# A decoder layer on one core: TensorE's state sums, D product and x transposes move between the transposes of an attention group, and ScalarE alternates copies with exponentials

## The reference

```
x = layernorm(x + attention(x))              # 16 heads of 16, causal
x = layernorm(x + ssm(ctx, z=x))             # selective state space, DI = 256, 16 states
x = layernorm(x + moe(x))                    # 8 experts, top 2, INTER = 512
```

```
u     = silu(conv(in_proj @ ctx) + conv_b)
delta = softplus(dt_proj @ (x_proj @ u)[:8] + b);   B, C = (x_proj @ u)[8:24], [24:40]
state[e,n] = state[e,n] * exp(delta[e,t] * A[e,n]) + delta[e,t] * u[e,t] * B[n,t]
y[e,t]     = sum_n state[e,n] * C[n,t]  +  D[e] * u[e,t]
out        = y * silu(z)
```

## Time and profile before

| | us |
|---|---|
| median of 3 runs | 490.91 |
| lowest, highest | 488.83, 492.13 |
| the profiled execution | 490.96 |
| its span, from the first instruction to the last | 489.2 |

### The profile page before, as it was taken

One profiled execution on the slowest core, in us unless ns is written; L12 is line 12 of the kernel. 1 busy time (PEld: TensorE's weight loads), 2 busy tenths in 40 slices (PEclk: granted clock), 3 DMA queues, 4 the chain that ended last, 5 costly groups with the idle time before them and its releaser, 6 DMA issues.

```text
span 489.2 us, 5425 instructions
## 1 busy us (share of the span) xinstructions
PE 356.7 (73%) x1783; PEld 214.0 (44%) x1783; DVE 266.5 (54%) x392; ACT 200.6 (41%) x459; POOL 195.1 (40%) x155
## 2 busy tenths in 40 slices
PE   5990568786868978689586653149999999999800
PEld 3440434353434734347353331125666666666500
DVE  4036465769985897869986754622222222222246
ACT  2258666863756655575565500012222222222100
POOL 2030324579463776357645442031333333332111
PEclk9995667989887976889777975559999999999965
DMA  6002001015111241014210714610111111111052
GB/s 189 0 5 86 21 3 44 21 44 194 45 43 44 62 175 40 25 44 148 68 45 21 232 48 171 237 43 11 54 46 43 43 45 44 44 52 46 22 182 86
DMA packets 29437, 34.45 MB, mean 70 GB/s; under 512 B 4058, under 2 KB 23810, under 8 KB 29410
## 3 DMA queue, kind: packets, MB, share of 16 engines
q1 hardware_dynamic: 27202, 28.07, 17.9%
q0 software_dynamic: 2208, 6.03, 4.2%
HBM read 28.92 MB, written 5.18 MB: 70 GB/s over the span
## 4 chain that ended last, share of the span: by engine, by line
PE 63%; DVE 14%; ACT 13%; issue 4%; DMA 2%; POOL 1%; DVEq 1%; SPq 0%; POOLq 0%; ACTq 0%
PE psS L1354 17%; PE psT L1192 7%; PE psY L1146 5%; ACT probT L628 5%; PE psY L1373 4%; PE psO L1373 4%; PE psS L1064 3%; PE psO L1203 3%; DVE experts L813 3%; PE psS L1120 2%; PE psB L1364 2%; PE psS L1234 2%; ACT experts L588 2%; DVE negmax L820 2%; ACT probs_at L620 2%
## 5 line engine op out<-in xcount | busy, mean ns | idle before, releaser
L461 POOL TENSOR_TENSOR experts<-experts,c_rows 128x1024 f32<-128x1024 f32 x32 | 75.3, 2352 | 108.4 <-DVE experts L813 108.4
L1354 PE MATMUL psS<-experts,delta 128*128 x184 | 88.7, 606 | 0.5 <-ACT delta L707 0.5
L813 DVE TENSOR_TENSOR_SCAN experts<-experts 128x1024 f32<-128x1024 f32 x32 | 78.1, 2439 | 1.7 <-ACT experts L588 0.6
L1192 PE MATMUL psT<-ident,probs_at 128*128 128x128 f32 x192 | 38.9, 337 | 30.1 <-ACT probT L628 22.4
L508 POOL DMA_INDIRECT z_out<-delta,row_out x23 | 22.7, 988 | 90.9 <-ACT delta L721 90.9
L588 ACT ACTIVATE experts<-delta,A_sb 128x255 f32<-128x255 f32 x128 | 54.8, 521 | 2.2 <-DVE du L787 2.2
L998 DVE COPY u_sb<-psB 128x512 f32<-128x512 f32 x23 | 15.9, 692 | 68.6 <-PE psB L1364 68.6
L464 POOL TENSOR_TENSOR experts<-experts 128x512 f32<-128x512 f32 x32 | 49.9, 1559 | 2.5
L628 ACT COPY probT<-psT 128x512 f32<-128x512 f32 x48 | 28.1, 586 | 48.2 <-PE psT L1192 47.4
L1146 PE MATMUL psY<-experts,ident 128*128 128x512 f32 x64 | 41.6, 739 | 7.6 <-POOL experts L464 7.5
L1354 PEld LDWEIGHTS psS<-experts,delta 128*128 128x128 f32 x184 | 33.8, 195 | 25.3 <-issue 24.2
(11 more groups left out here) (209 smaller groups left out, 547.7 us busy)
## 6 DMA issues: line engine op xcount, KB each, us to landing
c_rows<-c_dram SPq DMA_DIRECT2D x32, 256.0 KB, 3.4
experts<-in_L_ffn_w_gate_dram SPq DMA_DIRECT2D x8, 512.0 KB, 5.9
experts<-in_L_ffn_w_up_dram SPq DMA_DIRECT2D x8, 512.0 KB, 6.8
experts<-in_L_ffn_w_down_dram SPq DMA_DIRECT2D x8, 512.0 KB, 7.8
x_in<-in_x_dram SPq DMA_DIRECT2D x4, 256.0 KB, 4.5
x_rows<-x_sb SPq DMA_DIRECT2D x4, 256.0 KB, 2.3
probs_at<-z_out SPq DMA_DIRECT2D x4, 256.0 KB, 4.2
c_rows<-z_out SPq DMA_DIRECT2D x4, 256.0 KB, 4.7
```

The costliest lines, as they stand in the source:

```text
L461: pool.tensor_tensor(states[:, g % ST], states[:, g % ST], c_rows[:, g % CR].rearrange("p n (o s) -> p n o s", o=1).broadcast_to([P, 2, HA ...
L813: dve.tensor_tensor_scan(states[:, g % ST].rearrange("p n h s -> p (n h s)"), dA[:, g % DA].rearrange("p n h s -> p (n h s)"), dBu[:, g % ...
L1192: ins = pe.transpose(psT[:, r * P:(r + 1) * P], probs_q[:, (GH * G + r) % PR, j * P:(j + 1) * P], ident[:])
L1354: ins = pe.matmul(psS[:, bank, :], xgT[:, s % 2, k, :], gate_up_of(bass.ds(e, 1), i)[:, k, :], start=(k == 0), stop=(k == FC - 1))
```

## The change

TensorE's list: the state sums of steps 0 to 3 no longer follow a group. In step 1 there is none; step 2 holds the sums of step 0 and step 1 in the two gaps between the three sets of transposes; step 3 has the sum of step 2 and the D product there, step 4 the sum of step 3 and the transposes of the next x, which stood in step 5. In steps 5 and 6 the sum comes ahead of the Q and the K projection. ScalarE's list: copies of transposes and exponentials alternate, so the first head's exponentials stand ahead of the second copy. VectorE's list: the addition of the gated output in step 3 comes right behind the scan. The D product no longer counts on y_ps, and the waits on it follow.

```diff
-            sp.wait_ge(y_ps, STEPS + B)
+            sp.wait_ge(y_ps, STEPS)
...
                     G = GROUPS * b + m
-                    if 1 <= m <= 4:
-                        take_probT(G - 1, 0)
-                        take_probT(G - 1, 1)
-                    if m < GROUPS:
-                        exponentials(G, 0)
-                    if 1 <= m <= 4:
-                        take_probT(G - 1, 2)
-                    if m < GROUPS:
-                        exponentials(G, 1)
-                        exponentials(G, 2)
+                    for r in range(GH):
+                        if 1 <= m <= 4 and r < 3:
+                            take_probT(G - 1, r)
+                        if m < GROUPS:
+                            exponentials(G, r)
                     if 1 <= m <= 4:
                         take_o(G - 1)
-                    if m < GROUPS:
-                        exponentials(G, 3)
                     if m == 0 and f >= 0:
                         half_tanh(f)
-                    elif m == 5:
-                        if f >= 0:
-                            take_x2T(f)
-                        if b + 1 < B:
-                            take_xT(b + 1)
+                    elif m == 4 and b + 1 < B:
+                        take_xT(b + 1)
+                    elif m == 5 and f >= 0:
+                        take_x2T(f)
...
-                    dve.wait_ge(y_ps, g - ST + 1 + (g - ST) // NP)
+                    dve.wait_ge(y_ps, g - ST + 1)
...
-                dve.wait_ge(y_ps, (NP + 1) * (b + 1))
+                dve.wait_ge(y_ps, NP * (b + 1))
...
+                    if m == 3 and f >= 0:
+                        add_gated(f)
                     if m < GROUPS:
                         maxima(GROUPS * b + m)
...
-                    elif m == 3 and f >= 0:
-                        add_gated(f)
...
-                if m == 0:
-                    for half in range(HALVES):
-                        ins = pe.matmul(psY[:, half * S:(half + 1) * S], diag_D[:, half], u_sb[:, b, half, :],
-                                        start=False, stop=False, skip_group_check=True)
-                    ins.then_inc(y_ps, 1)
+
+            def add_skip(b):
+                for half in range(HALVES):
+                    pe.matmul(psY[:, half * S:(half + 1) * S], diag_D[:, half], u_sb[:, b, half, :],
+                              start=False, stop=False, skip_group_check=True)
...
                     if 1 <= m <= 4:
-                        attend(GROUPS * b + m - 1)
-                    if m == 2 and f >= 0:
-                        transpose_gated(f)
+                        transpose_probs(G - 1, 0)
+                        if m > 1:
+                            sum_states(NP * b + m - 2 if m == 2 else g - 1)
+                        transpose_probs(G - 1, 1)
+                        if m == 2:
+                            sum_states(g - 1)
+                        elif m == 3:
+                            add_skip(b)
+                        elif m == 4 and b + 1 < B:
+                            pe.wait_ge(prob_rdy, GROUPS * GH * (b + 1))
+                            transpose_x(b + 1)
+                        transpose_probs(G - 1, 2)
+                        weigh_values(G - 1)
+                        if m == 2 and f >= 0:
+                            transpose_gated(f)
                     elif m == 5:
                         if f >= 0:
                             transpose_x2(f)
+                        sum_states(g - 1)
                         if b + 1 < B:
-                            pe.wait_ge(prob_rdy, GROUPS * GH * (b + 1))
-                            transpose_x(b + 1)
                             project_qk(b + 1, 0, psS[:, 1, :], q_ps)
                     elif m == 6:
                         if f >= 0:
                             route(f)
                         transpose_o(b)
+                        sum_states(g - 1)
                         if b + 1 < B:
                             project_qk(b + 1, 1, psS[:, 2, :], k_ps)
                         project_out(b)
-                    elif m == 7 and b + 1 < B:
-                        project_v(b + 1, psS[:, 3, :])
-                    if g > 0:
+                    elif m == 7:
+                        sum_states(g - 1)
+                        if b + 1 < B:
+                            project_v(b + 1, psS[:, 3, :])
+                    elif g > 0:
                         sum_states(g - 1)
```

9 lines of the change are left out of this document (3 added, 6 removed).

## The result

The kernel after took 473.83 us (median of 4 runs, 472.55 to 475.22), the one before 490.22 (4 runs beside it): a ratio of 0.966, interval 0.962 to 0.971. The forecast was 481.8 in a range of 475.0 to 488.5: the direction held, and the gain was 16.4 us where 9.2 were forecast, 1.2 us beyond the range.

What follows compares the result with a forecast made beforehand. No engine is always busy, so waits bound the loop: VectorE's about 51 of 228 us. Gains of 2.9 + 4.0 + 1.9 + 0.4 (batches 2, 1, 3, 0) = 9.2 us gave 481.8 us, range 475.0 to 488.5.

Steps and rivals of the forecast that it cites:

- the collision with GpSimd: Loop: VectorE scans slowed beside GpSimd's add, 4.8 us in the loop; taken as unchanged, 2 us to each side.
- Step 1: Batch 2: sum and D product leave it, scores start about 190.1 instead of 192.46; gain 1.5 us on VectorE.
- Step 2: Batch 2: two state sums in the gaps, clock rise at about 195, gated transposes done at 199.9 against 198.6.
- Step 3: Batch 2: VectorE reads gated output behind scan, after 1.9 wait; last exponential at 208.0 instead of 211.08; gain 3.1 us.
- Step 4: Batch 2: VectorE's wait of 3.43 falls to 1; x transposes and a sum lie in the gaps.
- Steps 5 to 7: Batch end: sums ahead of projections; from step 3's last exponential to next batch 20.25 us, was 20.0; batch nets 2.9.
- given back at the end of the batch: Rival, 0.15: attention output later by the sum ahead of it (1.02) and step 4's filled gaps; 487.4 us.
- Batch 1: Second batch: high clock already in step 2, so nothing from steps 1 and 2; 4.0 us from step 3 on.
- Batch 0: First batch: step 2 gains 1.5, its two-sum group gives back about as much, earlier x transposes half a microsecond; 0.4 us.
- The clock stays up: Rival, 0.20: TensorE at the high level from step 2 on and in the last batch's projection; 5 more, 476.8 us.
- Slower, by half rate: Rival, 0.10: clock low until step 4, filled gaps cost 7.0 a batch against 3.1 won; about 502 us.

## Why the prediction was right in its sign and too small

**The places were right.** Most of what it named is in the trace: line 864 behind scan and transposes, T0 of step 3 no longer waiting for it, the waits for scores and transposed outputs down (to 19.5 us, forecast 36), the wait for the attention output up, the granted clock at 0.93 where it was 0.52 from 205 to 212 (1.00 was forecast). Not so the waits for a copied bank, "mostly gone" in the forecast: 13.3 of 22.4 us are left. The mark it set for being wrong, batch 1 gaining less than batches 2 and 3, came true (1.5 against 5.3 and 4.8), and so the working has to be faulted batch by batch. Its errors are +3.6, -2.5, +2.4 and +2.9 us, together the 6.4 that the loop gained beyond the 9.2. Of the terms of its sum, two were wrong and matter most: the work of step 2 was taken too long, which left a wait in step 3, and the collision with GpSimd was left out in step 4.

**Step 1: direction right, the gain of 1.5 too small.** The first maxima came 3.9 us behind the step's multiply (183.65 less 179.77) where it was 6.1 before, so 2.3 were gained. The forecast had 4.7. The scores took longer than it allowed, 2.6 until VectorE saw them rather than 1.9, but they started 1.25 us into the step and not 2.8, right behind the products with V and without a wait. This made step 2 of batch 2 6.06 long instead of 6.9.

**Step 2: this is the step that failed.** "I take the rise later, at about 195, in the first sum": in the times of the trace of before that is 7.7 us into VectorE's step. It came 3.6 to 4.4 us into the step in all three batches, 2.4 us behind the start of the scores in batch 2. The prediction called the place unreadable and took 195 as the likeliest, between 192 and never; the run lies beyond the early end (192 is 4.7 into the step). So both sums ran at 1.02, the group had no waits, and the gated transposes were done 3.3 us behind the start of step 3's multiply instead of 5.7. Counted from the multiply of step 2 they were done at 9.3 instead of 12.6. Of that, 1.5 is the earlier start of the scores (step 1, above), and about 1.7 is left for the clock and the group without waits.

**Step 3: the wait of 1.9 that the forecast kept did not exist.** It was step 2's error handed on: the gated transposes ended before the scan. Step 3 took 8.15, and the forecast's times make it about 10.3. This is the largest term, 2.1 us in batch 2. The kernel with the early addition alone has no wait there either and gains 9 us, about the forecast's whole sum. That is luck and no support for the sum. What it does show is that the addition can start right behind the scan, and that the earlier scores and the filled gaps add another 7 us to it, where the forecast had 9.2 for all of them together.

**Step 4: the forecast gained 2.4 there (8.06 to 5.6) and 0.6 came.** This is the term that was not costed. The prediction held the collision with GpSimd to be a matter of scans, took "unchanged", and gave it 2 us to each side. The normalisation of step 4, 0.73 before, took 2.55; moving it gave 6.2 us of median (5.7 by the ratios). Had that term stood in the sum, the forecast would have been smaller yet: two errors of opposite sign partly covered each other.

The Trainium skill, SBUF — State Buffer, on the shared port pair, has VectorE and GpSimd lock each other out for whole instructions. The runs agree, more strongly than the prediction took it: the scan of 4.37 that ends 2.15 behind GpSimd's product, and the add of 3.13 instead of 1.26 that had to wait for the scan.

**Steps 5 to 7: net zero was forecast, and the net was mixed.** Step 5 gained 0.3 to 2.5 and step 6 up to 1.4. Step 7 lost 2.5, 3.1 and 1.3, in each batch by a longer scan, in batch 0 also by the sum waiting for a GpSimd that was itself held up, and in batch 1 by sum and K projection at the low clock. The rival "given back at the end of the batch" had the place and the direction; it had the attention output late by the sum's own 1.02, while the sum's wait for GpSimd (1.90 in batch 0) was in nobody's working. Restoring the old place of the sums changed nothing measurable unless GpSimd was relieved too.

**Batch 1: 4.0 forecast, 1.5 came.** The forecast reasoned that batch 1 had the high clock before and so would only gain in steps 3 and 4. It gained 1.4 and 1.6 there, but its step 2 now began at the low level as the others did (5.75 to 6.66), and step 7 lost 3.1.

**Batch 0: 0.4 forecast, 4.0 came.** The clock was different: 0.75 over 74 to 84 us before, 1.00 over 74 to 82 after; step 2 went from 10.82 to 7.59. Step 5 went from 8.11 to 5.65, and step 7 gave 2.5 back. A part of it is not the change's own. Up to step 2 of this batch, eight of the kernels run here have the very lists of after, and the step took 7.57 to 9.41 us in them, of which 0 to 7 us at the low level. So a single profiled execution can be off by 1.8 us, and that of after was at the lucky end. With the old placing the step took 8.8 to 11.4.

**The rivals.** "The clock stays up" (476.8) came nearest. It was right that the clock would be high from within step 2 on; it was wrong in the last batch, where the sum ahead of the output projection took 2.03 and the projection 2.72 (1.89 at the high level), and the wait for the attention output is still 5.6 us. "Slower, by half rate" has no trace: every sum between transposes of steps 2 and 3 took 1.02, in all four batches. Half rate did come back in step 4, where that sum took 1.71 to 1.92 in batches 1 to 3. What it cost there was not measured by itself. But its side remark, that a scan would wait for its state bank, is what costs 12.0 us once the sums leave the gaps.

**What stays open.** The clock's share of the 16.4 us can't be parted from that of the order, since TensorE's order also moves the low stretches; where the clock was raised by itself the gain was given back. The profiled executions say something on step 2 of batches 1 to 3. At the high level throughout, it took 5.75 us with the old placing (batch 1 of before) and 5.60 with the new one and the added products: no difference to speak of. With 3.3 to 4.4 us of it at the low level, it took 7.8 to 8.5 with the old placing and 6.1 to 6.7 with the new one. So the emptied step 1 mostly makes step 2 bear a low clock better. But this compares kernels, not one edit. Why the clock falls where it does in one batch and not in the next, in the same order of instructions, is open as well.

## What to carry to other kernels

Where an engine works through its list in order and waits again and again for a short copy, independent work belongs into those gaps rather than behind the group. Here that paid only together with an emptied step 1, whose work went into them. And follow every ring that this work feeds, since here a sum that moved back by a step held up the recurrence for 12 us and cost more than half of the gain. Test the parts of such a change in both directions: the early addition gave 9 us alone and nothing on top of the rest, because both removed the same wait. Once waits of VectorE disappear, look at what GpSimd starts at that moment: two instructions moved from behind the scan to ahead of it were worth more than any other single move tried on top of the change.

## What the runs showed of the hardware

- VectorE's scan and GpSimd's product or add, where they met, ran one after the other: a scan of 2.29 us took 4.37, an add of 1.26 took 3.13. VectorE's `tensor_scalar` normalisation, with one tensor input, was held up as well (two instructions of 0.73 together took 2.55, and 3.53 in one kernel).
- In step 2 of batch 2 the granted clock rose to the 2.4 GHz level about 2.4 us after the scores started; it had been there from 176.6 to 179.8 and fell behind a wait of TensorE of 1.32 us, which ended at 179.10. TensorE worked without a break from there to the rise. Two products that nobody reads, placed in the idle time of step 0, only moved the low stretch. Two placed in the gaps of step 1 shortened it from 10 us to 3.3 in batches 1 and 3.
- Four float32 transposes take 0.60 to 0.66 us where the granted clock is at the high level and 1.06 to 1.12 at the low one, in every kernel of the study, with some sets between the two where the level changed.
